# GpSimd's gathers of a graph kernel: written out, with index columns read from the sorted edge rows

## The reference

```python
edge_index = jnp.stack([src, dst])
h = jnp.maximum(_layernorm(x, axis=-1), 0.0)
x = x + _L0_gnn_ref(h, edge_index, edge_weight)        # sum of sqrt(softmax_in * softmax_out) * h[src]
h = jnp.maximum(_layernorm(x, axis=-1), 0.0)
x = x + _L1_gnn_ref(h, src, dst, L1_gnn_beta)          # two layers of cosine attention, softmax over a node's edges
h = jnp.maximum(_layernorm(x, axis=-1), 0.0)
x = x + _L2_gnn_ref(h, L2_gnn_weight, src, dst, edge_type_16)   # sum of h[src] @ W[type], 16 types
h = jnp.maximum(_layernorm(x, axis=-1), 0.0)
x = x + _L3_gnn_ref(h, src, dst, edge_type_32, L3_gnn_basis, L3_gnn_coeff, L3_gnn_self_weight, L3_gnn_bias)  # mean of h[src] @ W[type], 32 types
```

## Time and profile before

| what | us |
|---|---|
| median of 3 runs (16192.64 to 16202.92) | 16194.08 |
| span of the profiled execution | 16122.9 |
| PE busy in it | 7118.7 (44%) |
| DVE busy | 6491.8 (40%) |
| ACT busy | 2663.4 (17%) |
| POOL busy | 9426.9 (58%) |

### The profile page before, as it was taken

One profiled execution on the slowest core, in us unless ns is written; L12 is line 12 of the kernel. 1 busy time (PEld: TensorE's weight loads), 2 busy tenths in 40 slices (PEclk: granted clock), 3 DMA queues, 4 the chain that ended last, 5 costly groups with the idle time before them and its releaser, 6 DMA issues.

```text
span 16122.9 us, 152937 instructions
## 1 busy us (share of the span) xinstructions
PE 7118.7 (44%) x35085; PEld 6087.1 (38%) x35140; DVE 6491.8 (40%) x18639; ACT 2663.4 (17%) x7299; POOL 9426.9 (58%) x9933
## 2 busy tenths in 40 slices
PE   4311111232332566666656666665444444333333
PEld 1100001222222565666656566665333333233333
DVE  3322224333333455555555555554333333222222
ACT  0000000000000333333433333333000000000000
POOL 4476673666666555555545555554666665666666
PEclk5555555555555555555555555555555555555555
DMA  1000001111111111111121121112112122111111
GB/s 29 3 5 5 4 5 43 22 22 22 22 22 22 34 38 40 39 39 41 38 38 44 45 46 44 44 44 38 39 42 43 41 43 47 28 24 24 23 24 23
DMA packets 429662, 499.75 MB, mean 31 GB/s; under 512 B 235856, under 2 KB 245584, under 8 KB 417584
## 3 DMA queue, kind: packets, MB, share of 16 engines
q0 software_dynamic: 317504, 279.59, 11.9%
q1 hardware_dynamic: 97730, 214.09, 3.9%
q10 hardware_dynamic: 14316, 4.81, 0.2%
HBM read 397.49 MB, written 94.54 MB: 31 GB/s over the span
## 4 chain that ended last, share of the span: by engine, by line
DVE 27%; another core or an unknown queue 24%; issue 23%; DVEq 19%; PE 6%; SPq 0%; POOL 0%; ACT 0%; DMA 0%; ACTq 0%; POOLq 0%
DVEq L1371 7%; DVE pay_d L1371 6%; DVE pay_d L1221 5%; DVEq L420 4%; DVE ps L1170 2%; DVE ps L1161 2%; DVE pd L1103 2%; DVE prod L1156 1%; DVE Z L1149 1%; DVEq L1221 1%; PE ps L1568 1%; PE ps L1581 1%; DVE Z L1146 1%; DVE Z L1209 1%
## 5 line engine op out<-in xcount | busy, mean ns | idle before, releaser
L685 POOL DMA_INDIRECT Z<-table,idx x4986 | 4717.0, 946 | 3913.4 <-issue 1662.4
L1581 PE MATMUL ps<-Z 128*128 128x65 f32 x9972 | 2330.5, 416 | 4323.2 <-DVE Z L1209 1546.2
L1581 PEld LDWEIGHTS ps<-Z 128*128 128x128 f32 x9972 | 2203.3, 328 | 4562.5 <-issue 4417.2
L685 POOL DMA_INDIRECT Z<-table_a,idx x1662 | 1572.0, 946 | 945.2 <-issue 557.7
L661 POOL DMA_INDIRECT bins_dst<-slot_d x1612 | 1562.7, 969 | 960.8 <-issue 493.2
L685 POOL DMA_INDIRECT Z<-table_b,idx x1662 | 1571.9, 946 | 854.0 <-issue 535.0
L1371 DVE SCALAR_TENSOR_TENSOR pay_d<-pay_d,ps 128x65 f32 x4986 | 1111.2, 223 | 2365.7 <-issue 1884.6
L1568 PE MATMUL ps<-Z 128*128 128x65 f32 x6648 | 1528.1, 417 | 176.6 <-DVE pay_d L1221 113.7
L1535 PE MATMUL ps<-pay_d,Z 128*128 x6648 | 1535.9, 421 | 62.0 <-ACT Z L744 37.5
L1568 PEld LDWEIGHTS ps<-Z 128*128 128x128 f32 x6648 | 1475.7, 332 | 231.4 <-DVE pay_d L1221 110.9
L1535 PEld LDWEIGHTS ps<-pay_d,Z 128*128 128x128 f32 x6648 | 1486.5, 333 | 64.2 <-issue 63.9
(11 more groups left out here) (245 smaller groups left out, 7970.7 us busy)
## 6 DMA issues: line engine op xcount, KB each, us to landing
pay_d<-locals_ SPq DMA_DIRECT2D x92, 1152.0 KB
Z<-table,idx POOLq DMA_INDIRECT x4986
table_b<-pay_d SPq DMA_DIRECT2D x192, 256.0 KB
Z<-table_a,idx POOLq DMA_INDIRECT x1662
Z<-table_b,idx POOLq DMA_INDIRECT x1662
bins_dst<-slot_d POOLq DMA_INDIRECT x1612
table_a<-kept SPq DMA_DIRECT2D x94, 256.0 KB
slot_d<-pay_d SPq DMA_DIRECT2D x62, 91.0 KB
```

The costliest lines, as they stand in the source:

```text
L685: nc.gpsimd.indirect_dma_start(rows[:, at.slot, j, 0:width], None, ps_.table, bass.IndirectOffsetOnAxis(ap=idx[:, at.slot, j:j + 1], axis= ...
L1581: last = mm(p_pair[:, at.three, j * ROW:(j + 1) * ROW], hot_d[:, at.three, j, :], given, start=True, stop=True)
```

## The change

The tile `idx` and the semaphores `idx_ready` and `gathers_started` go away, and with them ACT's copies. The Pool's gathers are written out by a loop of Python, 277 groups for each of five passes (8310 gathers and 1385 waits), with constant numbers in the waits. Each gather reads its 128 indices from the field of `pdi` that its pass uses. The Pool waits once for the load of `pd` ahead of the first pass. In ACT's list of steps an empty step keeps the offset 5.

```diff
-        idx = sb("idx", [P, RING, ITEMS], I32)
...
-        idx_ready = sem("idx_ready")
-        gathers_started = sem("gathers_started")
...
         @block.gpsimd
         def _(pool):
-            pool.sem_inc(gathers_started, CREDIT)
...
             def gather(ps_):
                 used = msg_made if ps_.scaled else summed
                 width = ROW if ps_.softmax else D
-
-                def fetch(at):
-                    n = ps_.gather + at.g
-                    u = at.g + (ps_.gather if ps_.scaled else ps_.every)
-                    pool.wait_ge(idx_ready, done(n))
+                for g in range(NG):
+                    slot = g % RING
+                    u = g + (ps_.gather if ps_.scaled else ps_.every)
                     pool.wait_ge(used, done(u - RING))
-                    pool.sem_inc(gathers_started, 1)
                     for j in range(ITEMS):
                         nc.gpsimd.indirect_dma_start(
-                            rows[:, at.slot, j, 0:width], None, ps_.table,
-                            bass.IndirectOffsetOnAxis(ap=idx[:, at.slot, j:j + 1], axis=0)).then_inc(gathered[at.slot], 16)
-                run_pass(pool, [(0, fetch)])
-
+                            rows[:, slot, j, 0:width], None, ps_.table,
+                            bass.IndirectOffsetOnAxis(ap=pdi[:, g * ITEMS + j, ps_.column:ps_.column + 1], axis=0)).then_inc(gathered[slot], 16)
+
+            pool.wait_ge(bins_loaded_d, 16)
...
         @block.scalar
         def _(act):
-            act.sem_inc(idx_ready, CREDIT)
...
-                def rows_wanted(at):
-
-                    act.wait_ge(gathered[at.slot], ps_.gathers(at) * (16 * ITEMS))
-                    nc.scalar.copy(idx[:, at.slot, :], pdi[:, bass.ds(at.g * ITEMS, ITEMS), ps_.column]).then_inc(idx_ready, 1)
...
-                steps += [(RING - 1, rows_wanted), (-2, idle)]
+                steps += [(RING - 1, idle), (-2, idle)]
```

## The result

The changed kernel takes 15991.5 us (median of 4 runs, 15968.7 to 16014.8) beside 16198.5 us for the kernel before: a ratio of 0.987, with an interval of 0.9853 to 0.9887. Two later comparisons gave 0.990 (0.9879 to 0.9922) and 0.9869 (0.9845 to 0.9893). The forecast was 16124.1 us, 0.43% faster; the gain is 1.0 to 1.3%, so the direction was right and the size about a third of what came.

What follows compares the result with a forecast made beforehand. It took the Pool to be halted by a full ring, waiting for its consumers. From 16122.9 us of span, -34, -8, -18 and -10 gave 16052.9; with 71.2 outside it, 16124.1 us (0.43% faster); range 15960 to 16285.

Steps and rivals of the forecast that it cites:

- Pass 3: In 46 halts the Pool restarts 0.6 us sooner without ACT's copy: taken -18 us, bounds 0 and -28.
- After a halt: Pool code from release to first gather: one wait fewer saves 0.05 us at some 200 halts, -10 us (0 to -40).
- Pass 0: Late copies end 42 halts; only their hand-over tail, 0.8 us each, is saved: -34 us, bounds 0 and -238.
- Passes 1 and 2: The copy comes with the release; 0.1 us for each of 80 halts in pass 2: -8 us, bounds 0 and -16.
- ACT's copies: ACT no longer makes 1385 copies, 262.6 us beside other engines' work: taken 0, bounds 0 and -55 us.
- Loop and branch: The Pool's loop registers and backward branch go; the branch was taken as already hidden between groups, so 0 us.
- Code: The Pool's written-out list, 0.6 MB more, is fetched ahead of use: taken 0, bounds 0 and 213 us for unhidden refills.
- (A): Rival: nothing changes, the `used` wait takes the copy's place; 16176 to 16194 us; chance 0.24 together with (E).
- (E): Rival: the Pool's halts last as long because another wait, not the copy, was last; time as (A), joint chance 0.24.
- (B): Rival: the late copies in pass 0 do bound; all gains give 15873 us, half of them 16030; chance 0.12.
- (C): Rival: without halts for copies the Pool's bursts get longer and slow DVE; +128 us, 16322 us; chance 0.13.
- (D): Rival: the strided index operand costs 23 ns per gather; +191 us, 16385, a third 16260; chance 0.07 with code loading.

Runs made afterwards that it cites:

- e12: The changed kernel with the count-up of `gathers_started` put back between the Pool's wait and its gathers: 16084.4 us, 0.9952 of the kernel before.
- e1: The kernel before with its loop and count-up, but the index ring filled only once and no wait for later copies: 0.9947 of the kernel before.
- e11: The changed kernel run once more with no edit, beside the kernel before on the same chip: 15941.2 us, 0.9869 of the kernel before.
- e2: The kernel before with the gathers written out and the count-up dropped, ACT's copies and the wait for them kept: 0.9939 of the kernel before.
- e3: The changed kernel with ACT's copies made but unread, and ACT waiting for its own copy of six groups before: 0.9996 of the kernel before.
- e5: The changed kernel with two Pool memsets ahead of each group in passes 0, 3 and 4: pass 3 +34 us, pass 4 +22 us, pass 0 -66 us.

## Why the prediction was right or wrong

**What bounds the kernel**: the rows were read rightly as far as they go (gathers every 1.25 us, consumers that don't wait for gathers, a chain without the Pool), and the halts are indeed set by the consumers' signals. What was missed is that the consumers weren't at work either. The earlier trace rows were taken for DVE being slow; the timeline above shows a whole set of signals late. That the Pool "waits for the consumers" was true of the signal and not of the work.

**Pass 3**, -18 of at most -28 us forecast, -59 measured. One failed step is the reading of the earlier trace rows: the 0.6 us between DVE's start and the Pool's was put down to the copy. e12, which copies nothing, has 0.62 there, and in the earlier trace rows itself the Pool had passed its waits at 12410.4, before ACT's copy began. That price belonged to the count-up. The copy had a price too, in other halts: in 45 of the 69 it came last, 0.88 us behind the sums' signal (median), and e1 and e12 give 43 us for it where the forecast had 28 at most.

**After a halt**: "I take 0.05 for each of some 200 halts, -10 us, bounds 0 and -40". This is the term that was mis-sized, and the heart of the miss. It counts one wait fewer and leaves out the count-up, which no engine waits for, though it stood between the wait and the first gather. Of the 0.9 us from copy to gather that the prediction read in the earlier trace rows, 0.75 us is the time from the count-up's instruction to the gather. The count-up costs 0.53 us at a restart (0.62 against 0.09), there are 632 restarts in the profile before, not 200, and 143 us of time came of it (e12 against e11), 0.24 us for each of e12's 595.

**Pass 0**, -34 forecast, about -36 measured (means of two and three profiles): the right number by luck. If the tail of the late copies had been the gain, e1 and e12, which have no copies, would show it; they are 8 to 25 us slower than the kernel before. e2, which keeps the copies and drops the count-up, has about half of the gain (2554). That the late copies wouldn't give their 238 us was rightly seen: the wait for the messages took their place.

**Passes 1 and 2**, -8 forecast. Measured -31 (within its spread of 40) and -45. Of pass 2, e2 and e12 have 15 and 18 us and e1 none. The 0.1 us of the earlier trace rows was the right price for the copy's lateness, but the count-up's 0.5 us after more than 200 halts in each of these passes was left out.

**ACT's copies** at 0, bounds 0 and -55: open, as e3 and e2 disagree. **Loop and branch** at 0: borne out by e1 and e12 (0.9947, 0.9952). The prediction's remark that each of 230 backward branches would have a price holds only where the target isn't at hand, and it is near: one turn of the loop is 58 instructions of the Pool in the trace. **Code** at 0 of at most 213 us: borne out, with the Trainium skill ("Runtime: NRT & Kernel Launch", Instruction fetch mechanics) on the long list read ahead: the code queues brought 1.75 MB in place of 1.26, 0.49 MB more beside the 0.6 worked out, and no halt can be put down to it. **Index columns** at 0: borne out, 943 ns for a gather. The Trainium skill's section 7 of "GPSIMD Engine Reference", half as much again for steps over 8 bytes, doesn't reach a gather's index column by this number.

**Rivals.** (A) and with it (E) fell. (B) has nearly the right size (half of it: 16030) for a wrong reason. (C), that bursts of gathering hold the others up, has its mechanism borne out by e5, where DVE's slow stretches are gone, and by the semaphores' updates, but not its sign: pass 3 got shorter bursts by the change, three groups and not four. That this comes of the sooner restart is likely but not shown. (D) fell. Of the signs, DVE's "issue" time ahead of its sums in pass 4 was to stay at 728 us and fell to 551; pass 0 changed by less than 100 us, which said nothing of the miss, as it lay elsewhere.

## What to carry to other kernels

Count every instruction between a wait and the work behind it, also one that nobody waits for: it is on the path each time the wait is the last to end, here 0.5 us some 600 times, of which somewhat less than half reached the total. Read the idle times of the other engines in a halt: when three of them start within 0.1 us, after nothing has run for 10 us, look at when the producer ended; here it wasn't late but its signal was. And where a limit takes the place of work, a cheap test is to add work in the halts: if the time stays, the halt was a rest and not a wait; but test it on more than one chip.

## What the runs showed of the hardware

- On the slower chips, signals of PE came late while the Pool gathered on: 11 and 14 us after its work in the halt shown, and over 5 us for 180 of 274 groups of pass 3. In that halt they were let go 3.6 us after the last gather. On the faster ones, an engine started 0.1 us after PE's end. The kernel before takes 16150 us on the first kind and 12805 to 12815 us on the second, at the same granted clock (0.50) and the same busy times.
- On the slower chips six gathers took at least 8.5 us in passes 3 and 4, against the Pool's 7.5 us, with all, a quarter of the bytes or half of the rows. The gathers' packets kept 1.2 us behind the Pool all the same, on both kinds of chip.
- An indirect gather of 64 rows takes the Pool 900 ns, one of 128 rows 944 ns: the time is nearly all per gather.
- A semaphore instruction of its own ahead of a gather, a count-up or a second wait, takes 17 ns in the trace, and the gather starts 0.74 to 0.80 us behind it. Without it, the gather starts 0.09 to 0.26 us after the signal. From DVE's start on the same signal it is 0.62 us with the count-up and 0.09 without.
